# Compressed interaction network on one core: layer 1's products read both operands from SBUF, and layer 2's PSUM ring goes from five banks to six

## The reference, cut to what matters

```python
e = stack([tbl_f[ids[:, f]] for f in range(39)], axis=1)             # [1024, 39, 16]
def layer(x0, xk, W, b):
    return relu(einsum('bhd,bmd,shm->bsd', xk, x0, W) + b[None, :, None])
x1 = layer(e, e, W1, b1)          # W1 [128, 39, 39]
x2 = layer(e, x1, W2, b2)         # W2 [128, 128, 39]
h = concatenate([x1.sum(-1), x2.sum(-1), dense_ctx], axis=1)         # [1024, 272]
y = relu(relu(h @ W_top1 + b_top1) @ W_top2 + b_top2) @ W_top3       # [1024, 1]
```

## Time and profile before

| | us |
|---|---|
| three runs, median | 1172.12 (1167.8 to 1173.06) |
| the profiled execution | 1171.53 |
| its span | 1169.7 |
| TensorE matmul busy | 1089.3 |
| VectorE busy | 981.9 |
| GpSimd busy | 850.0 |
| ScalarE busy | 822.2 |
| granted TensorE clock, mean over the span | 0.999 |

### The profile page before, as it was taken

One profiled execution on the slowest core, in us unless ns is written; L12 is line 12 of the kernel. 1 busy time (PEld: TensorE's weight loads), 2 busy tenths in 40 slices (PEclk: granted clock), 3 DMA queues, 4 the chain that ended last, 5 costly groups with the idle time before them and its releaser, 6 DMA issues.

```text
span 1169.7 us, 18115 instructions
## 1 busy us (share of the span) xinstructions
PE 1089.3 (93%) x4475; PEld 824.1 (70%) x4475; DVE 981.9 (84%) x2893; ACT 822.2 (70%) x2774; POOL 850.0 (73%) x951
## 2 busy tenths in 40 slices
PE   0069999999999999999999999999999999999998
PEld 0037677677777777767777667777777777777687
DVE  4048999998988989998998668998899989996787
ACT  5027677777777777777777667777777777775774
POOL 7756888878787888788878758787887864543454
PEclk9999999999999999999999999999999999999999
DMA  6178678685877678684876538776787858665342
GB/s 182 29 161 182 123 145 179 147 168 106 188 163 147 135 154 180 145 168 100 195 162 150 110 70 189 167 145 130 154 185 154 168 110 201 146 147 104 73 85 52
DMA packets 82881, 166.61 MB, mean 142 GB/s; under 512 B 17812, under 2 KB 31014, under 8 KB 82775
## 3 DMA queue, kind: packets, MB, share of 16 engines
q0 software_dynamic: 28272, 85.81, 42.2%
q1 hardware_dynamic: 54502, 79.64, 24.3%
HBM read 78.36 MB, written 3.81 MB: 70 GB/s over the span
## 4 chain that ended last, share of the span: by engine, by line
PE 83%; DVE 9%; POOL 3%; issue 2%; SPq 1%; ACT 1%; DMA 1%; DVEq 0%; ACTq 0%
PE bank L821 66%; PE l_acc L806 14%; DVE acc L680 4%; POOL emb L404 3%; DVE t_sum L688 1%; PE misc L854 1%; PE misc L850 1%; DVE p2acc L698 1%; DVE x1l L645 0%; DVE p L721 0%; SPq L359 0%; DVE t_sum L692 0%; ACT prod L527 0%; DVE p1acc L655 0%; SPq L366 0%
## 5 line engine op out<-in xcount | busy, mean ns | idle before, releaser
L527 ACT ACTIVATE prod<-bank,emb 128x128 f32<-128x128 f32 x2552 | 715.8, 380 | 272.0 <-PE bank L821 269.5
L680 DVE SCALAR_TENSOR_TENSOR acc<-bank,emb,acc 128x128 f32<-128x128 f32 x2184 | 612.5, 345 | 68.1 <-PE bank L821 67.3
L821 PE MATMUL bank<-w2h,x1h 128*128 128x512 f32 (+1 forms) x1280 | 537.0, 420 | 10.4 <-DVE acc L680 8.2
L821 PE MATMUL bank<-w2l,x1h 128*128 128x512 f32 (+1 forms) x1280 | 494.4, 386 | 0.0
L821 PE MATMUL bank<-w2h,x1l 128*128 128x512 f32 (+1 forms) x1280 | 449.7, 417 | 0.0
L404 POOL DMA_INDIRECT emb<-tbl,idx x312 | 312.5, 1001 | 82.5 <-issue 77.9
L821 PEld LDWEIGHTS bank<-w2h,x1h 128*128 128x128 f32 x1280 | 241.0, 188 | 106.3 <-issue 44.7
L821 PEld LDWEIGHTS bank<-w2h,x1l 128*128 128x128 f32 x1280 | 240.6, 188 | 74.2 <-issue 20.3
L821 PEld LDWEIGHTS bank<-w2l,x1h 128*128 128x128 f32 x1280 | 241.0, 188 | 61.1 <-issue 22.1
L424 POOL TENSOR_TENSOR tree<-prod 128x640 f32<-128x640 f32 x127 | 237.2, 1868 | 55.0 <-DMA prod<-prod 55.0
L415 POOL DMA_DIRECT2D prod<-prod x127 | 123.6, 973 | 170.2 <-ACT prod L527 170.1
(11 more groups left out here) (105 smaller groups left out, 421.4 us busy)
## 6 DMA issues: line engine op xcount, KB each, us to landing
prod<-prod POOLq DMA_DIRECT2D x127, 640.0 KB
z<-e_rows SPq DMA_DIRECT2D x96, 234.0 KB
z<-e_rows SPq DMA_DIRECT2D x192, 78.0 KB
z<-e_rows SPq DMA_DIRECT2D x96, 156.0 KB
emb<-tbl,idx POOLq DMA_INDIRECT x312, 4.9
prod<-w_by_h SPq DMA_DIRECT2D x3, 832.0 KB, 8.4
z<-e_rows SPq DMA_DIRECT2D x32, 66.0 KB
e_rows<-e_t SPq DMA_DIRECT2D x8, 256.0 KB
```

Source lines behind the costliest of these rows:

```text
L527: last = nc.scalar.activation(prod[:, ct % P_RING, i, n * S:(n + 1) * S], bank[:, (ct * NB + k) % RING, n * S:(n + 1) * S], ACT.Copy, scal ...
L680: nc.vector.scalar_tensor_tensor(dst, src, scale, dst if step else b2_row[:, :], ALU.mult, ALU.add).then_inc(v_step, 1)
L821: last = nc.tensor.matmul(out_bank[:, 0:b - a], x, w[:, a:b], start=(n == 0), stop=(n == 2))
```

## The change

`e_rep` and both copies to it go. VectorE's products read the repeated rows and `rest` where the DMAs put them, in SBUF, and wait for those DMAs themselves. The bank that this frees makes the ring six. The tail's small tiles are placed by the ring's order.

```diff
-FIRST_AT = 38
-SWAP_AT = 4
-REP_AT = 26
-RING = 5
+RING = 6
...
-        e_rep = ps("e_rep", [P, CH])
...
-        tail1 = [e_rep[:, 0:P], l1_acc[:, 0:P], bank[:, 0, 0:P], bank[:, 1, 0:P]]
-        tail3 = bank[:, 4, 0:P]
-        tail2 = [bank[:, 2, 0:P], bank[:, 3, 0:P]]
+        tail_bank = [bank[:, (CTS * NB + n) % RING, 0:P] for n in range(RING)]
+        tail1 = [tail_bank[0], l1_acc[:, 0:P], tail_bank[1], tail_bank[2]]
+        tail2 = tail_bank[3:5]
+        tail3 = tail_bank[5]
...
@@ load_shifted (SyncE)
                 wait(sp, f_used, NF * (f - 1))
-                wait(sp, rep_ready, f - 1)
+                wait(sp, f_made, NF * (f - 1))
...
@@ ScalarE: copy_rep and copy_first, and the three places that call them, are gone
-                nc.scalar.copy(e_rep[:, :], z[:, f % 2, NF, :]).then_inc(rep_ready, 1)
-                nc.scalar.copy(e_rep[0:3 * N_REST, :], rest[0:3 * N_REST, :].bitcast(F32)).then_inc(first_ready, 1)
...
@@ make_f (VectorE)
                 if t == REST:
                     dve.wait_ge(in_second[f % 2], 64 * (f // 2 + 1))
-                    if direct(f):
-                        dve.wait_ge(in_first, 64 * (f + 1))
-                        first = rest[0:rows, :].bitcast(F32)
-                    else:
-                        dve.wait_ge(first_ready, f - f // CPT - 1)
-                        first = e_rep[0:rows, :]
-                    nc.vector.tensor_tensor(part, first, part, ALU.mult).then_inc(f_made, 1)
+                    dve.wait_ge(in_first, 64 * (f + 1))
+                    nc.vector.tensor_tensor(part, rest[0:rows, :].bitcast(F32), part, ALU.mult).then_inc(f_made, 1)
                     return
-                dve.wait_ge(rep_ready, f + 1)
+                if t == 0:
+                    dve.wait_ge(in_rep[f % 2], 64 * (f // 2 + 1))
                 for k, ts in enumerate(Z_GROUPS):
                     if t == ts[0]:
                         dve.wait_ge(in_z[f % 2][k], Z_LOADS[k] * (f // 2 + 1))
-                nc.vector.tensor_tensor(part, e_rep[0:rows, :], part, ALU.mult).then_inc(f_made, 1)
+                nc.vector.tensor_tensor(part, z[0:rows, f % 2, NF, :], part, ALU.mult).then_inc(f_made, 1)
...
@@ mlp_tail (TensorE)
-                    if o >= 2:
-                        wait_bank_free(pe, CTS * NB + o - 2)
+                    if o != 1:
+                        wait_bank_free(pe, CTS * NB + max(o - 1, 0))
...
-                for n in range(2, RING):
+                for n in range(3, RING):
```

More of the change, by code:

```diff
@@ L238, in build @@
         in_marks, w_rest_high, w_rest_mixed = sem("in_marks"), sem("w_rest_high"), sem("w_rest_mixed")
-        rest_high, rest_mixed, first_ready = sem("rest_high"), sem("rest_mixed"), sem("first_ready")
+        rest_high, rest_mixed = sem("rest_high"), sem("rest_mixed")
         back_staged, w1_summed = sem("back_staged"), sem("w1_summed")
         w2h_cast, w2_staged, w2l_made = sem("w2h_cast"), sem("w2_staged"), sem("w2l_made")
-        lifted, et_ready, rep_ready = sem("lifted"), sem("et_ready"), sem("rep_ready")
+        lifted, et_ready = sem("lifted"), sem("et_ready")
         f_made, f_used = sem("f_made"), sem("f_used")
@@ L496, in copy_lifted @@
                     nc.scalar.copy(e_t[:, 0:4, :], misc[:, :].rearrange("p (k n) -> p k n", k=4)).then_inc(et_ready, 1)
-            def copy_rep(f):
-                act.wait_ge(in_rep[f % 2], 64 * (f // 2 + 1))
-                wait(act, f_made, NF * f if direct(f) else NF * f + 1)
-                nc.scalar.copy(e_rep[:, :], z[:, f % 2, NF, :]).then_inc(rep_ready, 1)
-            def copy_first(f):
-                act.wait_ge(in_first, 64 * (f + 1))
-                act.wait_ge(f_made, NF * f)
-                nc.scalar.copy(e_rep[0:3 * N_REST, :], rest[0:3 * N_REST, :].bitcast(F32)).then_inc(first_ready, 1)
             def round_rest(f):
@@ L574, in _ @@
             copy_lifted(0, 1)
-            copy_rep(0)
             for c in range(-1, CHUNKS):
@@ L584, in _ @@
                         copy_lifted(c // CPT + 1, LIFT_COPY_AT.index(g))
[L585 to L590, removed]
                     if c in BATCH_IN:
```

## The result

The changed kernel takes 1186.22 us (median of 6 runs, 1182.61 to 1194.06), the kernel before 1169.96 us beside it (6 runs, 1164.40 to 1173.17). The ratio is 1.0144, 95% interval 1.0117 to 1.0170: slower by 1.4%, some 17 us. The profiled execution took 1188.04 us, its span 1186.2, against 1171.53 and 1169.7: 16.5 us more of each.

What follows compares the result with a forecast made beforehand. TensorE bounds most chunks, VectorE close behind. Longer VectorE products add 1.04 us to each of 26 chunks, +27 us on 1171.5, other terms 0: forecast 1198 us, own range 1182 to 1225, 8 in 10 within 1163 to 1240.

Steps and rivals of the forecast that it cites:

- The mechanism: VectorE instructions with two SBUF operands and GpSimd's additions get in each other's way; those with a PSUM operand do not.
- a stall ends with one GpSimd instruction: Rival: a product waits only for the addition under way, 0.26 us each; 1165 to 1178 us, middle 1172; chance 0.18.
- The products' stalls: 215 products get two SBUF operands and stall 0.39 us each beside GpSimd's additions: 2.6 us a chunk.
- VectorE's busy time: In the 26 chunks of the two long stretches: 30.23 + 2.6 + 0.1 = 32.9 us a chunk.
- The chunk: Each of 26 chunks goes from 32.86 to 33.9 us, with 1.0 of VectorE idle rest: +27 us in all.
- The sum rule: A chunk is the longer of TensorE's 32.2 us and VectorE's busy time plus some rest.
- the second rival: Products miss GpSimd's additions, the ring decides: 1160 us, chance 0.10; holds below about 0.15 us of stall a product.
- The sixth bank: TensorE runs some 0.8 us longer before a stalled VectorE holds it; 0 to 17 us possible, 0.1 a chunk counted.
- GpSimd at 0: A product holds GpSimd up to 0.68 us, four or so times a chunk, but GpSimd has room: 0.
- +12 ns for a product: A stall-free product with two SBUF operands takes 694 ns against 682 with PSUM: 2.6 us, 0.1 a chunk.
- The copies, SyncE's wait, the loads: ScalarE's copies going (33.3 us of its time), SyncE's changed wait and products waiting for loads of `rest`: 0 each.
- The tail and the tower's chunks: Batch chunks and the two behind them have VectorE room, the tail has the same instructions: 0.

Runs made afterwards that it cites:

- m_lock: Separate test, no model: 20 VectorE products of 128x512 per phase, SBUF or PSUM operands, beside GpSimd additions or transfers; two-SBUF products waited at most 1375 ns, PSUM ones took at most 692.
- m_queue: Separate test, no model: two-SBUF VectorE products beside GpSimd turns of transfer issue and addition; longest 12.66 us, 1.83 with a memset and wait between issue and addition.
- the fence: Memset and wait between GpSimd's transfer issue and next addition: kernel before 1181.97 us against 1184.84 beside it, ratio 0.9975; changed kernel 1191.44 us, ratio 1.0058.
- b_merge26: Kernel before with VectorE's merge steps at g = 26, 27, 28 instead of 22, 27, 29: 1170.53 us, ratio 0.9991.
- b_rest_sbuf: Kernel before with only the 23 REST products reading their first operand from SBUF, those copies gone, other copy and five banks kept: 1194.42 us, ratio 1.0224.
- b_merge29: Kernel before with VectorE's merge steps at g = 26, 27, 29 instead of 22, 27, 29: 1175.23 us, ratio 1.0053.

## Why the prediction was right, and where its sizes were off

Slower was right, and 1186.2 lies within 1163 to 1240 and the forecast's own 1182 to 1225. The size was too large: +27 us forecast, 16.5 in the profiled execution, and that the two are so near is in part luck. The 27 were for the 26 chunks of the two long stretches, and these lost 11.1. The other 5.4 came where the forecast had 0: the first chunk, the stretches with the tower's batches, and the tail. A part of both is the lower clock, for which the sum has no term.

- **The mechanism** (both-SBUF instructions and GpSimd's additions keep each other out, instructions with a PSUM operand are left alone) is shown: by the products before and after, by the cut additions, and by m_lock. It is too narrow in one point: line 696, with one SBUF operand and none in PSUM, was held too, to 2658 ns. As the Trainium skill ("SBUF — State Buffer", "Who interferes with whom") has it, an instruction with two SBUF inputs contends with a GpSimd one that reads SBUF, and m_lock agrees with its one-instruction wait (1375 ns at most). The 3.5 us of the kernel and the 12.66 of m_queue go beyond that rule. So the rival "a stall ends with one GpSimd instruction" is right for an addition that comes alone and wrong for this kernel's queue; with the fence it became true there as well.
- **The products' stalls**, 0.39 us each, were a little too long. 224 both-SBUF products take 183.2 + 41.5 = 224.7 us, over 224 x 0.682 = 152.8 by 71.9: 0.32 each (0.27 for the six, 0.61 for REST).
- **VectorE's busy time** is the term that was mis-sized: 32.9 us a chunk forecast, (123.54 + 371.93 + 318.61) / 26 = 31.31 measured, +1.08 instead of +2.7. I added the new stalls to the old ones. The old ones shrank: the merge and mix instructions lost 15.1 + 5.6 + 4.5 us, and line 696 went from 5.6 to 3.4 us. A probable reading is that an addition that met a product, or was held by one, is no longer there for the next; it was not tested apart.
- **The chunk** came out at 865.58 / 26 = 33.29 us, not 33.9. The idle rest is 2.0, not 1.0. VectorE's waits for GpSimd are 0.5 of it at most. The 1.0 came from three disturbed chunks and was set against the mean of all, where the rest was 32.86 - 30.23 = 2.6 before already, since a quiet chunk leaves 3.9 free. The sum rule behind it (chunk = VectorE's busy time + a rest) is refuted by the runs: the twelve chunks in the middle took 12.5 us more of VectorE at no cost, b_merge26 freed 40 us and gained nothing on balance, b_rest_sbuf added 7 and lost 2.2%. What fits them is that single late moments against the ring's depth decide, and that a stop of TensorE brings the lower clock behind it. (The point that the second rival turns on does not follow from the terms either: (32.86 - 1.0 - 30.33) / 6.7 is 0.23 us a product, not 0.15.)
- **The sixth bank** was taken at 2.6 us. With the missing copies it is worth 5.8 where nothing stalls; alone, in the presence of stalls, about 4, not resolved.
- **GpSimd at 0** was wrong. GpSimd's busy time rose by 52 us, and VectorE waited 15.4 us for it. Most of that lies in the first four chunks (5.5 us of the loss, the 1.7 of the lower clock among them). That a product which goes first holds an addition is the likely reason; no run takes it apart. "Busy 435.61 of 529.30" was an average over a queue whose work must be done in time, not only done.
- **+12 ns for a product** was wrong: the median after is 681, and the same nine products that had 694 before have 680. Where the 12 came from is not shown. The 65 ns less that the prediction worked out from the Trainium skill ("VectorE: DVE Perf Modes", "The TRN2 errata") are not seen either.
- **The copies, SyncE's wait, the loads** at 0 were right: TensorE's wait for ScalarE went from 3.6 to 3.7, and the only wait for a load of `rest` is 2.2 us in the first chunk, 2.0 before. ScalarE is busy 799.6 us and not 789.
- **The tail and the tower's chunks** at 0 were not: 4.7 us more stand there, an unknown part of it by the 6.8 us at the lower clock in the tail.

## What to carry to other kernels

Before an operand is moved from PSUM to SBUF, count the VectorE instructions that will then read SBUF twice, and see what GpSimd reads at those times: a PSUM operand, even one that costs a copy, buys freedom from GpSimd. Price a stall by its longest single case against the depth of the buffer behind it and by who else waits on it, not by adding it to an engine's total. Where GpSimd both issues transfers and computes, put a wait between the issue and the next computing instruction and measure: in the kernel before it cut the longest instruction from 3.6 to under 2 us and gained 0.25%, in the changed one it gained more but left GpSimd late. And count a stop of TensorE at more than its length, where its clock falls behind it.

## What the runs showed of the hardware that was not expected

- Beside turns of a transfer's issue and an addition that is ready behind it, one both-SBUF product of VectorE took 12.66 us (six turns); with the addition not yet ready during the issue, 1.83 us at most. Neither issues one at a time (606 ns from product to product) nor additions alone (1375 ns of wait) do it.
- A product with one PSUM operand took 677 to 692 ns beside continuous additions.
- An instruction with a single operand, in SBUF (line 696), took 2658 ns once beside GpSimd's issue and additions, and 419 in the median.
- Four stops of TensorE, of 2.3 to 3.0 us (one in the changed kernel, three in b_merge29), were each followed by 3.4 us at a granted clock of 0.50, with 9 or 10 matmuls in them; the 3.5 us behind one had 18.
- Moving three merge steps freed 40 us of an engine that is busy 84% and moved the time by 0.1%, within the interval of no change: what it gained, the steps' new places took back.
